# A causal convolution split into three float32r matmuls, inside a one-core conv and gated FFN kernel

## The reference

```
K = 2 * einsum('hn,hnl->hl', Ct, exp(dtA * l)).real      # 512 taps for each of 32 channels
y = irfft(rfft(x) * rfft(K))[..., :512] + x * D           # causal convolution over the 512 steps
y = y * (step < length)
gate = q8(y) @ gate_w.T ;  up = q8(y) @ up_w.T            # 512 -> 1376
x + q8(silu(gate) * up) @ down_w.T                        # 1376 -> 512
```

## Time and profile before

| | |
|---|---|
| median of 3 runs | 321.7 us (321.67 to 321.93) |
| the profiled execution | 321.68 us |
| its span | 319.9 us |
| TensorE matmuls busy | 308.4 us, 96% |
| weight loads busy | 162.0 us, 51% |
| VectorE busy | 187.3 us, 59% |
| ScalarE busy | 161.3 us, 50% |
| granted TensorE clock | 0.999 |

### The profile page before, as it was taken

One profiled execution on the slowest core, in us unless ns is written; L12 is line 12 of the kernel. 1 busy time (PEld: TensorE's weight loads), 2 busy tenths in 40 slices (PEclk: granted clock), 3 DMA queues, 4 the chain that ended last, 5 costly groups with the idle time before them and its releaser, 6 DMA issues.

```text
span 319.9 us, 4409 instructions
## 1 busy us (share of the span) xinstructions
PE 308.4 (96%) x1561; PEld 162.0 (51%) x1587; DVE 187.3 (59%) x408; ACT 161.3 (50%) x222; POOL 13.7 (4%) x25
## 2 busy tenths in 40 slices
PE   1999999999999999999999999999999999999996
PEld 0467655554455554555455544555455554444443
DVE  6977588475637664465634756375744747433443
ACT  3924556364545364464635546453643646644550
POOL 3031000000001000000001000010001000010010
PEclk9999999999999999999999999999999999999999
DMA  6879999400005570078202680066500770070018
GB/s 200 190 190 230 275 321 328 164 1 2 0 0 101 161 264 2 0 131 299 96 0 36 164 326 0 0 110 235 182 0 0 134 262 0 2 132 0 0 22 243
DMA packets 14013, 38.40 MB, mean 120 GB/s; under 512 B 1470, under 2 KB 6558, under 8 KB 11052
## 3 DMA queue, kind: packets, MB, share of 16 engines
q1 hardware_dynamic: 8412, 26.61, 23.6%
q0 software_dynamic: 5584, 11.57, 20.8%
HBM read 33.93 MB, written 15.81 MB: 155 GB/s over the span
## 4 chain that ended last, share of the span: by engine, by line
PE 93%; DVE 3%; DMA 2%; issue 1%; DVEq 0%; SPq 0%
PE up_ps L588 23%; PE gate_ps L588 23%; PE y_ps L512 22%; PE down_ps L526 17%; PE down_ps L629 1%; PE down_ps L542 1%; PE y_ps L542 1%; PE y_ps L629 1%; DMA toep<-kpad_scratch 1%; DMA prm<-in_params 1%; PE down_ps L466 1%; PE gate_ps L554 1%; PE up_ps L554 1%; DMA kpad_scratch<-hq 1%; DVE xt L902 0%
## 5 line engine op out<-in xcount | busy, mean ns | idle before, releaser
L882 DVE SCALAR_TENSOR_TENSOR hv<-sil,fac,up_ps 128x512 f32<-128x512 f32 (+1 forms) x88 | 65.6, 746 | 116.5 <-PE up_ps L588 86.1
L413 ACT ACTIVATE sil<-gate_ps,fac 128x512 f32<-128x512 f32 (+1 forms) x88 | 60.4, 686 | 128.3 <-PE gate_ps L588 122.5
L588 PE MATMUL up_ps<-yq,wu 128*128 128x512 bf16 (+3 forms) x367 | 88.6, 363 | 0.3
L588 PE MATMUL gate_ps<-yq,wg 128*128 128x512 bf16 (+3 forms) x366 | 88.2, 363 | 0.6 <-DVE hv L882 0.3
L512 PE MATMUL y_ps<-xt,toep 128*128 128x512 f32 (+3 forms) x256 | 80.4, 434 | 0.2 <-DMA toep<-kpad_scratch 0.2
L526 PE MATMUL down_ps<-wd,hq 128*128 128x512 bf16 (+1 forms) x251 | 65.4, 379 | 0.7
L512 PEld LDWEIGHTS y_ps<-xt,toep 128*128 128x128 f32 x256 | 47.2, 190 | 21.5 <-issue 2.9
L588 PEld LDWEIGHTS gate_ps<-yq,wg 128*128 128x128 bf16 x372 | 36.2, 100 | 40.0 <-issue 1.7
L588 PEld LDWEIGHTS up_ps<-yq,wu 128*128 128x128 bf16 x372 | 36.3, 100 | 38.3
L394 ACT ACTIVATE hq<-hv 128x1024 uint16<-128x1024 uint16 (+1 forms) x48 | 46.8, 975 | 0.0
L526 PEld LDWEIGHTS down_ps<-wd,hq 128*128 128x128 bf16 (+1 forms) x264 | 25.9, 98 | 32.5 <-issue 12.6
(11 more groups left out here) (148 smaller groups left out, 99.8 us busy)
## 6 DMA issues: line engine op xcount, KB each, us to landing
xt<-in_xT SPq DMA_DIRECT2D x8, 1024.0 KB, 7.5
out<-in_x SPq DMA_DIRECT2D x7, 1024.0 KB, 5.7
out<-res POOLq DMA_DIRECT2D x7, 1024.0 KB, 7.8
toep<-kpad_scratch SPq DMA_DIRECT2D x6, 1024.0 KB, 10.0
toep<-kpad_scratch SPq DMA_DIRECT2D x8, 256.0 KB, 3.8
wd<-in_down POOLq DMA_DIRECT2D x1, 1280.0 KB, 22.3
xt<-in_x SPq DMA_DIRECT2D x1, 1024.0 KB, 7.4
out<-xt SPq DMA_DIRECT2D x3, 256.0 KB, 3.8
```

What stands on the lines that cost most here:

```text
L413: nc.scalar.activation(sil[b][0:w, :], gate_ps[b][0:w, :], ACT.Silu, scale=fac[0:w, S_GATE:S_GATE + 1]).then_inc(silu_done, 1)
L588: mm = nc.tensor.matmul(ps[b][0:w, cols], wt[:, k, c * P:c * P + w], yq[par][:, version, k, cols], start=(k == 0), stop=(k == LB - 1))
L882: v.scalar_tensor_tensor(hv[c // 2 % 3][0:w, c % 2], sil[b][0:w, :], fac[0:w, S_UP:S_UP + 1], up_ps[b][0:w, :], ALU.mult, ALU.mult).then_i ...
```

## The change

From block 1 on the convolution's distances 0, 1 and 2 are no longer one float32 matmul each but three float32r matmuls: high taps times high x, high taps times low x, low taps times high x. float32r is a 4-byte type of which the matmul uses fewer bits of the mantissa. The high parts (`th`, `xh`) are written by ScalarE as copies into float32r tiles, the low parts (`tl`, `xl`) by VectorE as the float32 value less the high part. The table has two channels (a pair) at a time: 128x1024 for x, 128x768 for the taps of distances 0 to 2. The distance 3 stays one float32 matmul. Block 0 keeps the float32 form.

`HIGH_PLAN` puts ScalarE's copies of a pair of block g + 2 into slots 4 and 5 (pair 0) and 8 and 9 (pair 1) of block g, and VectorE's subtractions into slots 5 and 6, and 9 and 10. In the part ahead of the slots the copies and subtractions of block 1 stand between the treatments of block 0's channels, and its two convolutions stand one `by_channel` later. SyncE's loop over blocks is written out, and a block's loads stand ahead of the copy of x to the output.

```diff
+SHORT = L - P
+        th = [sb(f"th{i}", [P, 2, SHORT], F32R) for i in range(2)]
+        tl = [sb(f"tl{i}", [P, 2, SHORT], F32R) for i in range(2)]
+        xh = [sb(f"xh{i}", [P, 2, L], F32R) for i in range(2)]
+        xl = [sb(f"xl{i}", [P, 2, L], F32R) for i in range(2)]
...
-            with sp.Fori(0, (NBLK - 4) // 2) as j:
-                for par in range(2):
-                    at_least(sp, added[par], 16 * (j + 1))
-                    copy_x(2 * j + 2 + par, par)
-                    next_conv(2 * j + 4 + par, par)
+            for g in range(NBLK - 2):
+                if g + 3 < NBLK:
+                    sp.wait_ge(y_ready, HB * (g + 2))
+                    load_x_t(g + 3, (g + 3) % 2)
+                    load_toep(g + 3, (g + 3) % 2)
+                if g:
+                    sp.wait_ge(added[(g - 1) % 2], 16 * ((g - 1) // 2 + 1))
+                copy_x(g + 1, (g + 1) % 2)
...
+            def high_x(g, par, half, pair):
+                at_least(act, xt_in[par], 16 * (half + 1))
+                at_least(act, y_ready, HB * (g - 1) + 2 * pair + 2)
+                nc.scalar.copy(xh[pair][:], xt[par][:, 2 * pair:2 * pair + 2]).then_inc(x_high, 1)
+            def high_taps(g, par, half, pair):
+                at_least(act, conv_in[par], 16 * half)
+                at_least(act, y_ready, HB * (g - 1) + 2 * pair + 2)
+                nc.scalar.copy(th[pair][:], toep[par][:, 2 * pair:2 * pair + 2, 0:SHORT]).then_inc(taps_high, 1)
...
                     if ahead and c in CODE_PLAN:
                         code_y(g + 1, 1 - par, CODE_PLAN[c])
+                    if ahead == 2 and c in HIGH_PLAN:
+                        high_x(g + 2, par, half + 1, HIGH_PLAN[c])
+                    if ahead == 2 and c - 1 in HIGH_PLAN:
+                        high_taps(g + 2, par, half + 1, HIGH_PLAN[c - 1])
...
                 for d in distances:
-                    last = nc.tensor.matmul(y_ps[h % 2][:, d * P:L], toep[par][:, h, d * P:(d + 1) * P],
-                                            xt[par][:, h, 0:L - d * P], start=(d == 0), stop=(d == 2))
+                    cols, rest = slice(d * P, (d + 1) * P), slice(0, L - d * P)
+                    if d == 3:
+                        nc.tensor.matmul(y_ps[q][:, 3 * P:L], toep[par][:, h, cols], xt[par][:, h, rest],
+                                         start=False, stop=False)
+                        continue
+                    for n, (taps, xs) in enumerate(((th, xh), (th, xl), (tl, xh))):
+                        last = nc.tensor.matmul(y_ps[q][:, d * P:L], taps[pair][:, q, cols], xs[pair][:, q, rest],
+                                                start=(d == 0 and n == 0), stop=(d == 2 and n == 2))
...
             by_channel(0)
-            conv(1, 1, 0, 0, [0, 1, 3, 2])
             by_channel(1)
-            conv(1, 1, 0, 1, [0, 1, 3, 2])
+            conv(1, 1, 0, [0, 1, 3, 2])
             by_channel(2)
+            conv(1, 1, 1, [0, 1, 3, 2])
             by_channel(3)
...
+            def low_x(g, pair):
+                at_least(dve, x_high, 2 * (g - 1) + pair + 1)
+                v.tensor_tensor(xl[pair][:], xt[g % 2][:, 2 * pair:2 * pair + 2], xh[pair][:].bitcast(F32),
+                                ALU.subtract).then_inc(x_split, 1)
...
                     if ahead and c in FINISH_PLAN:
                         finish_y(g + 1, 1 - par, FINISH_PLAN[c])
+                    if ahead == 2 and c - 1 in HIGH_PLAN:
+                        low_x(g + 2, HIGH_PLAN[c - 1])
+                    if ahead == 2 and c - 2 in HIGH_PLAN:
+                        low_taps(g + 2, HIGH_PLAN[c - 2])
...
+HIGH_PLAN = {4: 0, 8: 1}
```

More of the change, by code:

```diff
@@ L498, in _, with conv_first, conv @@
             warm(WARM[3])
-            def conv(g, par, half, h, distances):
+            def conv_first(h):
+                pe.wait_ge(toep_first[h], 16)
+                if h == 0:
+                    pe.wait_ge(xt_in[0], 16)
+                at_least(pe, yv_done, h - 1)
+                for d in (0, 1, 3, 2):
+                    last = nc.tensor.matmul(y_ps[h % 2][:, d * P:L], toep[0][:, h, d * P:(d + 1) * P],
+                                            xt[0][:, h, 0:L - d * P], start=(d == 0), stop=(d == 2))
+                last.then_inc(y_ready, 1)
+            def conv(g, par, h, distances):
                 m = HB * g + h
+                pair, q = h // 2, h % 2
                 if distances[0] == 0:
[L504 to L509, removed]
+                    at_least(pe, x_split, 2 * (g - 1) + pair + 1)
+                    at_least(pe, taps_split, 2 * (g - 1) + pair + 1)
                     at_least(pe, yv_done, m - 1)
                 for d in distances:
-                    last = nc.tensor.matmul(y_ps[h % 2][:, d * P:L], toep[par][:, h, d * P:(d + 1) * P],
-                                            xt[par][:, h, 0:L - d * P], start=(d == 0), stop=(d == 2))
+                    cols, rest = slice(d * P, (d + 1) * P), slice(0, L - d * P)
[6 more added lines that the diff above has]
+                                                start=(d == 0 and n == 0), stop=(d == 2 and n == 2))
                 if d == 2:
@@ L557, in by_channel, with beside @@
                             mm.then_inc(ready, 1)
-            def beside(g, par, half, c, down, ahead):
+            def beside(g, par, c, down, ahead):
                 for step, h, distances in CONV_PLAN.get(c, ()):
                     if step <= ahead and (down or (step, h) != (1, 1)):
-                        conv(g + step, (par + step) % 2, half + (1 if step == 2 else par), h, distances)
+                        conv(g + step, (par + step) % 2, h, distances)
                 if down and not ahead:
@@ L567, in beside, with slots @@
                     down_part(g - 1, 1 - par, c)
-            def slots(g, par, half, down, ahead):
+            def slots(g, par, down, ahead):
                 for c in range(CH):
@@ L581, in slots @@
                             if c == 0 and hi == HB:
-                                beside(g, par, half, c, down, ahead)
+                                beside(g, par, c, down, ahead)
                             if c == 0:
@@ L592, in slots @@
                     if c or not down:
-                        beside(g, par, half, c, down, ahead)
+                        beside(g, par, c, down, ahead)
             for h in range(HB):
-                conv(0, 0, 0, h, [0, 1, 3, 2])
+                conv_first(h)
             k_of(2)
@@ L926, in _ @@
             scale_y(0, 0)
-            for h in range(HB):
-                if h < HB - 1:
-                    scale_y(0, h + 1)
-                bound_y(0, 0, h)
-                finish_y(0, 0, h)
+            scale_y(0, 1)
+            bound_y(0, 0, 0)
+            finish_y(0, 0, 0)
+            low_x(1, 0)
+            scale_y(0, 2)
+            bound_y(0, 0, 1)
+            finish_y(0, 0, 1)
+            low_taps(1, 0)
+            scale_y(0, 3)
+            bound_y(0, 0, 2)
+            finish_y(0, 0, 2)
+            bound_y(0, 0, 3)
+            finish_y(0, 0, 3)
+            low_x(1, 1)
             scale_y(1, 0)
+            low_taps(1, 1)
             dve.wait_ge(k_ready, 2 * len(K_GROUPS))
```

53 lines of the change are left out of this document (32 added, 21 removed).

## The result

| | before | after |
|---|---|---|
| median | 321.8 us (321.67 to 321.93) | 326.5 us (325.30 to 327.86, 4 runs) |
| the profiled execution | 321.68 us | 325.30 us |
| its span | 319.9 us | 323.2 us |

The changed kernel is slower: 1.0148 times the kernel before, with 1.0106 to 1.0190 as the interval. 320.3 us was forecast, and 324.5 as the end of the range.

What follows compares the result with a forecast made beforehand. TensorE, streaming without a gap, was taken as the bound. Ahead of the slots 0, block 0 +2.0, blocks 1 to 5 5 x -0.47, block 6 -1.05, block 7 0: 321.7 - 1.4 = 320.3 us, range 316.0 to 324.5.

Steps and rivals of the forecast that it cites:

- I take the bf16 pace: TensorE's float32r matmuls: one bf16 pass each, so a channel costs 1.68 us, 0.48 less; 13.4 us over 28 channels.
- 4% eats the whole gain: Float32r matmuls: each tenth of pace above the bf16 one costs 4.1 us.
- TENSOR_TENSOR: VectorE's added subtractions: 1.22 us for 1024 elements and 0.95 for 768, 4.3 us per block.
- Slot 7 of a full block: TensorE waits there for VectorE's low taps, 1.45 us (1.1 to 1.8), so a full block gains 0.47.
- Block 0: Slot 7 there: split ready at 53.7, a TensorE wait of 3.9 us (3 to 5), block 0 loses 2.0.
- Ahead of the slots: The 0.96 us that block 1's channels 0 and 1 gain are spent in a wait: 0, with 0.5 either way.
- the fourth subtraction: Ahead of the slots: VectorE ends it at 35.3 and channel 2 of block 1 needs it, starting at 35.7 as before.
- ScalarE, SyncE's order, weight loads: ScalarE's 3.7 us of copies a block, SyncE's earlier loads and the added weight loads cost nothing.
- The clock: Rival, 20%: block 0's wait brings back the half clock, 1.6 us lost, at most 3; 322.3 us.
- The record's pace: Rival, 8%: float32r matmuls take two passes, a channel costs 0.97 us more than before; 358 us at most.
- no wait in slot 7: Rival, 8%: subtractions take half or stand where VectorE idles, so 12.4 us less, 309.3 us.

Runs made afterwards that it cites:

- the float32 channel: The changed kernel with channel 0 of block 2 alone computed by float32 matmuls from the unsplit tables: 321.38 us, 0.9989 of the kernel before.
- the bf16 tables: The changed kernel with its four split tables in bfloat16 instead of float32r, same order of instructions: one run, 322.49 us.
- the fastest kernel: Changed kernel with block 2's channel 0 in float32, pair 0's splits two slots earlier in blocks 1 to 5, its copies one later in block 0: 313.70 us.
- the two runs that moved it: Three fewer warm-up matmuls in the changed kernel, 325.26 us; three more in the kernel of 313.7 us, 315.34 us.

## Why the prediction was wrong

The direction was wrong, and the step that failed is the pace of the float32r matmul. "I take the bf16 pace" was argued from the number of passes; a channel was to save 0.48 us and saves 0.36. In the ruler's marks (where block 0 ends at its slot 9, so that 1.2 channels of its four count to the next stretch) the forecast was +2.55 for block 0, 5 x -0.47, and -1.6 for block 6: -1.4. Measured are +3.08, 0.0 and -1.06: +2.0. Of the 3.4 us between, 26 channels x 0.12 = 3.1 are the pace: the term "3 x (0.216 + 0.163 + 0.108) = 1.46" measured 1.57. (Two of the 28 stand ahead of the slots, where their gain is lost in a wait in any case.) The prediction gave the lever itself, "4% eats the whole gain", and the pace is off by 6.5% at 512 columns and 9% at 256; but it put the slow side on one far value, the record's two passes, and no chance on the few per cent between.

Point by point:
- *TENSOR_TENSOR* 1.22 forecast, 1.218 measured; the one of 768 elements 0.95 and 0.95.
- *Slot 7 of a full block* 1.45 forecast, 1.38 measured: right, as is its cause. With 1.44 gained and 1.38 lost the ruler shows 37.19 for 37.15, so a tenth stands in small gaps that I did not assign; without any wait a full block gains 1.34, so they go with the float32r matmuls and not with the splits.
- *Block 0.* TensorE ready at 49.76 forecast, 50.39 measured. It came only 0.33 earlier than before and not 0.96: 0.24 is the pace of two channels, and the rest was lost as the slots began: the gate matmuls at 37.31 waited 0.51 us for VectorE's product (0.34 before) and came 0.2 later than before, though the convolution just ahead of them had become shorter; the split there at 53.7 forecast, 53.9 measured. Two errors cancel in that: the silu of slot 5 did not stay at 46.17 but came at 46.85, behind the copy of x, and the chain took 6.3 and not 6.67 us. The wait was 3.7 for 3.9.
- *Ahead of the slots* 0 forecast, 0.2 measured, within the 0.5 given, but in this profile by luck. The wait for the fourth subtraction, ahead of channel 2, did not come: that subtraction ended at 34.86, and TensorE got there at 35.9. What had taken the two channels' gain was the stop of 0.86 us at 29.3, which was on no list. Where that stop was short or absent, TensorE did wait for `tl` there, 0.22 us with the float32 channel and 0.41 with the bf16 tables; so the forecast wait stood ready behind it.
- *ScalarE, SyncE's order, weight loads* nothing: right in the slots. The copy of the taps waited 1.28 us for the later DMA in block 0, behind VectorE's chain; loads of 190 ns did not bind at 256 columns, whose rows are 0.118 apart.
- *The clock* was a rival at 20% and 1.6 us. It came in 7 of 8 executions of the changed kernel, and the size was about right: 1.2 us in the one with a profile. I had it as another outcome; it is an addition to any outcome that has the wait.
- *The last store* was on no list: 1.3 us.
- *The record's pace*, a rival that did not come, adds up to 321.7 + 27 + 11 = 359.7 us and not to 358.

So for the median: 321.7 + 2.0 for the blocks + 1.3 for the last store + 1.2 for the clock = 326.2, of 326.5.

Two things that the prediction had right are what the experiments turned into time. All that TensorE saved went into six waits in slot 7 (4 x 1.38 + 1.20 + 3.7 = 10.4, against 28 x 0.36 = 10.1 us). The five of the full blocks were a matter of order alone: with the splits two slots earlier they are gone. Block 0's went when its channel needed no split; an earlier place for that split was not tried, and its table landed late (ScalarE stood 1.28 us for it). 313.7 us is what the float32r matmuls are worth at their real pace. The rival "no wait in slot 7" had said 309.3; with 0.36 for 0.48 on 26 channels it is 312.4, and the fastest kernel gives up one channel for float32.

## What to carry to other kernels

When a change buys time with one unshown price, ask at which value of it the sign turns, and give chances to values near that point, not only to the far end. A split that makes an engine's input needs its place in the maker's list where that engine idles, not where its user is near: here two slots decided 6.7 us. And one long wait of TensorE costs more than its length where the half clock comes back behind it.

## What the runs showed of the hardware

- A float32r matmul of 128 x 128 weights starts its follower after 0.230 us at 512 columns, 0.175 at 384 and 0.118 at 256; in bf16, in the same place, 0.216, 0.163 and 0.109. The Trainium skill, FP8 and Floating Point Precision, section TensorE Precision Notes, has the reduced form as a truncation of the 4 bytes that are read and gives no pace of it; one pass is what the trace shows, with 0.009 to 0.014 us more on each matmul.
- A subtraction with float32r output took VectorE 1.218 us for 1024 elements, where its float32 rows put 1.22, and 1.217 with bf16 output; a copy of 1024 elements to float32r took ScalarE 1.03 us, and the same to bf16.
- Behind a wait of 3.7 us the granted clock was 0.50 for some 3.4 us (in the profiled execution; by the mean clock in 7 of 8 executions of one kernel), so the same program has times 0.8 to 2.6 us apart; behind waits of 1.4 us in full blocks the mean stayed at 0.999 or more.
- A few instructions more in a program can slow its last store: with one more packet on the instruction queue, near the end, 64 KB took 3.2 to 3.4 us from issue to landing and not 2.0 to 2.1 (six profiles of each kind). That the fetch holds up the store is inferred from its time and from the two runs that moved it; how the two share the DMA engines was not seen.
- TensorE can stop in the middle of a group of matmuls with no semaphore between them, at a fixed number of its instruction list: 0.2 to 1.05 us, moved by six instructions when six were put in ahead of it. In two executions of one kernel it was 0.86 and 0.22 us.
